# A two-layer block in one persistent loop: three of four state blocks summed by VectorE, taps read from PSUM, norms applied by ScalarE

## The reference, cut to what matters

```python
# layer 0: attention with squared scores (16 heads of 16), then an int8-weight FFN (hidden 768)
A = (q_i @ k_i.T) ** 2 * mask;  o = (inter + A @ v) / (inter_z + A.sum(-1) + EPS);  x = o @ Wo
h = silu(x @ wg) * (x @ wu);    x = h @ wd
# layer 1: a state-space part in two directions r (forward and reversed sequence), 512 channels, 16 states n
u  = silu(conv4(x @ Win_u) + convb)                 # a causal convolution with 4 taps along time
dt = softplus(dtr @ Wdt + bdt)
h_t[n] = exp(dt_t * A[n]) * h_{t-1}[n] + (dt_t * u_t) * B_t[n]
y_t    = sum_n h_t[n] * C_t[n];   y = (y + u * D) * silu(z);  out = y @ Wout
# and a block-FP4 quantised FFN (hidden 704)
```

## Time and profile before

| | us |
|---|---|
| median of 3 runs (lowest, highest) | 6962.02 (6948.84, 6964.09) |
| the profiled execution, its span | 6966.85, 6965.1 |
| busy in the span: VectorE, TensorE, GpSimd, ScalarE | 5281.2, 5063.0, 4972.3, 4022.4 |
| share of the span: VectorE, TensorE, GpSimd, ScalarE | 76%, 73%, 71%, 58% |
| mean granted clock of TensorE | 0.803 |
| transfers: mean, share of the 16 DMA engines for the main queue | 44 GB/s, 13.5% |

### The profile page before, as it was taken

How to read it: one execution, slowest core, us unless ns; L and a number is a source line. 1 busy time by engine, 2 the same in 40 slices (tenths; PEclk the granted TensorE clock), 3 DMA queues, 4 the chain that set the end, 5 groups by cost and what they waited for, 6 DMA issues and landing times.

```text
span 6965.1 us, 83507 instructions
## 1 busy us (share of the span) xinstructions
PE 5063.0 (73%) x21853; PEld 3220.5 (46%) x21900; DVE 5281.2 (76%) x6580; ACT 4022.4 (58%) x6424; POOL 4972.3 (71%) x3786
## 2 busy tenths in 40 slices
PE   3776777868777686877868777676877768777665
PEld 2344444544444444544444444444544444444444
DVE  3277788787878778788787878878787787878884
ACT  1365665656656565655656656565665656656563
POOL 0177877777777777777778777777777777777894
PEclk6688888878878788887878878788887878888777
DMA  3011111111111111111111111111111111111110
GB/s 107 25 36 40 43 48 49 34 50 43 39 50 50 44 34 44 45 48 50 45 43 39 38 51 48 45 33 44 47 48 48 47 43 38 40 48 45 37 46 25
DMA packets 152821, 309.07 MB, mean 44 GB/s; under 512 B 20870, under 2 KB 58310, under 8 KB 149926
## 3 DMA queue, kind: packets, MB, share of 16 engines
q1 hardware_dynamic: 152278, 302.80, 13.5%
HBM read 285.90 MB, written 16.84 MB: 43 GB/s over the span
## 4 chain that ended last, share of the span: by engine, by line
PE 32%; issue 21%; DVE 17%; POOL 17%; ACT 10%; DMA 0%; DVEq 0%; POOLq 0%; SPq 0%; ACTq 0%
POOL arena_m L714 7%; PE psum L1310 7%; PE psum L1501 6%; DVE arena_m L1216 5%; POOL arena_m L725 5%; PE psum L1354 3%; DVE arena_m L1227 2%; PE psum L1273 2%; PE psum L1443 2%; PE psum L1481 2%; ACT hc L931 2%; ACT L759 2%; PE psum L1417 2%; PE psum L1389 1%; DVE arena_m L1156 1%
## 5 line engine op out<-in xcount | busy, mean ns | idle before, releaser
L714 POOL TENSOR_TENSOR arena_m<-bS,arena_m 128x512 f32<-128x512 f32 x2048 | 2703.6, 1334 | 394.7 <-PE psum L1501 358.7
L1216 DVE TENSOR_TENSOR_SCAN arena_m<-psum,arena_m 128x512 f32<-128x512 f32 x2048 | 2452.0, 1209 | 138.4 <-POOL arena_m L714 58.0
L923 ACT ACTIVATE psum<-arena_m,Aneg 128x512 f32<-128x512 f32 x2048 | 1414.8, 694 | 1387.1 <-DVE arena_m L1216 1355.7
L1501 PE MATMUL psum<-ident,arena_m 128*128 128x128 f32 x8192 | 1491.2, 317 | 858.2 <-DVE arena_m L1227 643.5
L725 POOL TENSOR_TENSOR arena_m<-arena_m,hc 128x512 f32<-128x512 f32 x1024 | 1362.9, 1331 | 821.1 <-ACT hc L931 766.5
L1501 PEld LDWEIGHTS psum<-ident,arena_m 128*128 128x128 f32 x8192 | 1121.2, 162 | 1563.4 <-issue 601.3
L1227 DVE SCALAR_TENSOR_TENSOR arena_m<-psum,Ct,arena_m 128x512 f32<-128x512 f32 x1024 | 746.4, 729 | 286.2 <-PE psum L1501 261.3
L1310 PE MATMUL psum<-arena_a 64*128 64x512 f32 (+3 forms) x2048 | 789.0, 517 | 98.7 <-ACT arena_a L790 49.3
L931 ACT ACTIVATE hc<-psum,Ct 128x512 f32<-128x512 f32 x1024 | 695.0, 679 | 229.4 <-PE psum L1501 172.8
L790 ACT ACTIVATE arena_a<-psum 128x384 f32<-128x384 f32 (+1 forms) x768 | 399.6, 526 | 356.1 <-PE psum L1310 352.4
L1310 PEld LDWEIGHTS psum<-arena_a 64*128 64x128 f32 x2048 | 382.9, 214 | 353.4 <-issue 217.1
(11 more groups left out here) (151 smaller groups left out, 7524.0 us busy)
## 6 DMA issues: line engine op xcount, KB each, us to landing
bS<-brow SPq DMA_DIRECT2D x512, 256.0 KB, 3.2
wB<-kept_B SPq DMA_DIRECT2D x16, 1408.0 KB, 6.8
wU<-kept_U SPq DMA_DIRECT2D x32, 512.0 KB, 4.3
wZ<-kept_Z SPq DMA_DIRECT2D x32, 512.0 KB, 4.5
wO<-kept_O SPq DMA_DIRECT2D x32, 512.0 KB, 4.8
wA<-kept_A SPq DMA_DIRECT2D x16, 768.0 KB, 7.0
wB<-kept_B SPq DMA_DIRECT2D x16, 768.0 KB, 4.2
wA<-kept_A SPq DMA_DIRECT2D x16, 640.0 KB, 4.0
```

Source lines behind the costliest of these rows:

```text
L714: pool.tensor_tensor(hb[s % HBS][:, m, :], bS[:, s % 2, :], du[r][:, m, :], ALU.mult).then_inc(m_dbu.sem, 1)
L923: act.activation(EB[j % EBS], dt[r][:, m, :], ACT.Exp, scale=Aneg[:, r, m, n:n + 1]).then_inc(m_dA.sem, 1)
L1216: dve.tensor_tensor_scan(v, EB[j % EBS], v, 0.0, ALU.mult, ALU.add).then_inc(m_scan.sem, 1)
L1501: ins = pe.transpose(HT[pos % 2][:, m * P:(m + 1) * P], hb[s % HBS][:, m, i * P:(i + 1) * P], ident[:, :])
```

## The change

1. *Blocks.* `ORDER` is gone; blocks 0, 1 and 2 of a state are added by VectorE from bank `i % 2`, block 3 is weighted by ScalarE and added by GpSimd.
2. *Taps.* The convolution has no `upad`. The taps read the PSUM bank of the product directly, shifted in the output, and the bank is free when the taps are done.
3. *Softplus.* Abs and Exp work in place in the PSUM bank, and VectorE's correction reads it there; the bank is free when that is done. `du` is made by GpSimd behind its two sums.
4. *Norms.* VectorE makes scale and shift ([128, 4] each), and ScalarE applies them, four instructions each.
5. *Query masks.* ScalarE makes all four. Both query products stand two batches ahead; the second is copied to `qraw` and masked in steps 27 and 28 (`a_qmask`).
6. *Table.* Most side work has new steps.

```diff
-    ORDER = (0, 2, 1, 3)
-        for j0, r, ahead, outs, res in ((0, 1, -1, (8, 9, 10, 11), (10, 12)), (HALF, 0, 0, (72, 74, 76, 78), (75, 79))):
+        for j0, r, ahead, outs, res in ((0, 1, -1, (8, 9, 10, 11), (10, 12)), (HALF, 0, 0, (74, 75, 77, 78), (76, 79))):
...
-        row("a_wo", None, 1, PE=[53, 54], DVE=[54, 55])
+        row("a_wo", None, 1, PE=[55, 56], DVE=[57, 58])
...
-        row("f_rest", None, 1, DVE=[60, 60, 61, 61])
+        row("f_rest", None, 1, DVE=[65, 65, 66, 66])
...
-            row("q_up", None, -1, first=2 * i, PE=[j + 3, j + 4], DVE=[j + 4, j + 5])
+            row("q_up", None, -1, first=2 * i, PE=[j + 3, j + 4], DVE=[j + 4, j + 6])
...
-        row("a_q", None, 2, PE=[125], ACT=[126], DVE=[126])
-        row("a_q", None, 1, first=1, PE=[28], ACT=[29], DVE=[29])
+        row("a_q", None, 2, PE=[125, 126], ACT=[126, 127])
+        row("a_qmask", None, 1, ACT=[27, 27, 28, 28])
...
+        for j0, j, r, ahead in ((13, 30, 1, 0), (97, 107, 0, 1)):
+            late = (0, 3, 6, 9) if r else (0, 2, 4, 6)
+            row("p_in", r, ahead, PE=[j0 + c for c in late], ACT=[j0 + c + 1 - r for c in late])
+            row("p_conv", r, ahead, DVE=[j0 + c + 2 - r for c in late for k in range(PAD)])
+            row("p_silu", r, ahead, ACT=[j0 + late[-1] + 4 - r])
+            late = (4, 7, 10, 13) if r else (4, 5, 6, 7)
+            row("p_dt", r, ahead, PE=[j + c for c in late], ACT=[j + c + 1 - r for c in late], DVE=[j + c + 2 - r for c in late],
+                POOL=[j + c + 3 for c in late])
...
-            "p_in": (1, lambda r, n: [(m_up, 2 * (NM * r + n + 1))]), "p_x": (2, lambda r, n: [(m_xd, r + 1)]),
-            "p_c": (1, lambda r, n: [(m_ct, r + 1)]), "p_dt": (1, lambda r, n: [(m_rl, NM * r + n + 1)]),
+            "p_in": (1, lambda r, n: [(m_conv, PAD * (NM * r + n + 1))]), "p_x": (2, lambda r, n: [(m_xd, r + 1)]),
+            "p_c": (1, lambda r, n: [(m_ct, r + 1)]), "p_dt": (1, lambda r, n: [(m_c2, NM * r + n + 1)]),
...
+                pool.wait_ge(*m_sum.by(b, 2 * q + 2))
+                pool.tensor_tensor(du[r][:, m, :], dt[r][:, m, :], u[:, m, :], ALU.mult).then_inc(m_du.sem, 1)
...
+            def norm(b, n, src, dst):
+                act.wait_ge(*ln_scale[n].by(b, 4))
+                for i in range(NT):
+                    act.activation(dst[:, i, :], src[:, i, :], ACT.Identity, scale=rstd[:, n, i:i + 1],
+                                   bias=shift[:, n, i:i + 1]).then_inc(ln_out[n].sem, 1)
...
-                act.activation(ex[:, c, :], src, ACT.Abs, bias=bdt[:, r, m:m + 1]).then_inc(m_ab.sem, 1)
+                act.activation(src, src, ACT.Abs, bias=bdt[:, r, m:m + 1]).then_inc(m_ab.sem, 1)
...
-                dve.scalar_tensor_tensor(u[:, m, :], upad[:, m % 2, tap:tap + T], convw[:, r, m, tap:tap + 1], u[:, m, :],
+                dve.scalar_tensor_tensor(u[:, m, late:T], src[:, 0:T - late], convw[:, r, m, tap:tap + 1], u[:, m, late:T],
                                          ALU.mult, ALU.add).then_inc(m_conv.sem, 1)
...
-                dve.scalar_tensor_tensor(yT[:, i, :], HT[0], Ct[:, r, i, n:n + 1], yT[:, i, :], ALU.mult,
+                dve.scalar_tensor_tensor(yT[:, i, :], HT[i % 2], Ct[:, r, i, n:n + 1], yT[:, i, :], ALU.mult,
                                          ALU.add).then_inc(m_y.sem, 1)
...
-                    if j % 2:
-                        yb, jy = spot(b, j - 5)
-                        if exists(yb):
-                            add_state(yb, jy // 2)
+                    yb, jy = spot(b, j - 5)
+                    if jy % NT < NT - 1 and exists(yb):
+                        add_state(yb, jy)
...
-                if pos % 2 == 0:
-                    pe.wait_ge(*m_y.by(b, c // 2))
+                if i == 1:
+                    pe.wait_ge(*m_hc.by(b, s))
                 else:
-                    pe.wait_ge(*m_hc.by(b, c // 2))
+                    pe.wait_ge(*m_y.by(b, 3 * s + (0, 0, 1, 2)[i]))
```

More of the change, by code:

```diff
@@ new lines, in block_kernel @@
+        row("a_wo", None, 1, PE=[55, 56], DVE=[57, 58])
+        row("f_stat", None, 1, DVE=[58, 59, 59], ACT=[60])
+        row("f_norm", None, 1, DVE=[61], ACT=[62])
+        row("f_turn", None, 1, PE=[63, 63], ACT=[64, 64])
+        row("f_rest", None, 1, DVE=[65, 65, 66, 66])
+        row("f_gate", None, 1, PE=[67, 67, 68, 68, 69, 70], ACT=[68, 68, 69, 69, 70, 71])
+        row("f_silu", None, 1, ACT=[70, 72])
+        row("f_up", None, 1, PE=[71, 72, 73, 74, 75, 76], DVE=[73, 73, 74, 75, 76, 77])
@@ L309, in block_kernel @@
+        row("f_down", None, 1, PE=[78, 80, 82, 84], DVE=[81, 86])
+        row("m_stat2", None, 1, DVE=[82, 86, 86], ACT=[87])
+        row("m_norm2", None, 1, DVE=[88], ACT=[89])
+        row("m_stat3", None, 1, DVE=[90, 90, 90], ACT=[91])
+        row("m_norm3", None, 1, DVE=[92], ACT=[93])
+        row("m_x", None, 1, POOL=[91])
+        row("m_turn", None, 1, PE=[94, 94], ACT=[95, 95])
         row("q_stat", None, -1, DVE=[20, 22, 23], ACT=[26])
-        row("q_norm", None, -1, DVE=[62, 63])
@@ new lines, in block_kernel @@
+            row("q_hquant", None, -1, first=QHEAD * i, DVE=[j + 6, j + 6, j + 6, j + 7, j + 7, j + 8])
+            row("q_htail", None, -1, first=QTAIL * i, POOL=[j + 8, j + 9, j + 9])
+            row("q_hturn", None, -1, first=2 * i, PE=[j + 10, j + 10], ACT=[j + 11, j + 11])
+            row("q_down", None, -1, first=i, PE=[j + 12], DVE=[j + 13])
+        for j, r, ahead in ((30, 1, 0), (107, 0, 1)):
+            row("p_x", r, ahead, PE=[j, j + 1], ACT=[j + 2])
+            row("p_rows", r, ahead, SP=[j + 3])
+            row("p_c", r, ahead, PE=[j + 4], DVE=[j + 5])
@@ L348, in block_kernel @@
-        row("a_v", None, 2, PE=[122, 123], DVE=[123, 124])
-        row("a_q", None, 2, PE=[125], ACT=[126], DVE=[126])
-        row("a_q", None, 1, first=1, PE=[28], ACT=[29], DVE=[29])
-        row("a_weigh", None, 1, PE=[j + 5 for j in UNIT])
+        row("a_k", None, 2, PE=[121, 122], ACT=[122, 123])
+        row("a_v", None, 2, PE=[123, 124], DVE=[125, 126])
+        row("a_q", None, 2, PE=[125, 126], ACT=[126, 127])
+        row("a_qmask", None, 1, ACT=[27, 27, 28, 28])
+        row("a_weigh", None, 1, PE=[j + 5 + (gu % NU == 0) for gu, j in enumerate(UNIT)])
@@ L778, in attn_q, with attn_qmask @@
                 act.wait_ge(*a_q_ps.by(b, h + 1))
-                for j in range(2):
+                if h:
+                    act.copy(qraw[:, :], bank("a_q", None, h)).then_inc(a_qr.sem, 1)
+                    return
+                for j in range(G):
                     act.activation(qm[:, j, :], bank("a_q", None, h), ACT.Copy, scale=qmask[:, j:j + 1]).then_inc(a_qa.sem, 1)
+            def attn_qmask(b, _, j):
+                act.wait_ge(*a_s_ps.by(b, NG * NU * G // 2 - G + j + 1))
+                act.wait_ge(*a_qr.by(b, 1))
+                act.activation(qm[:, j, :], qraw[:, :], ACT.Copy, scale=qmask[:, j:j + 1]).then_inc(a_qa.sem, 1)
             def square(b, _, w):
```

250 lines of the change are left out of this document (98 added, 152 removed).

## The result

| | us |
|---|---|
| before, median of 3 runs | 6962.02 (6948.84 to 6964.09) |
| after, median of 3 runs | 7215.55 (7205.03 to 7242.28) |
| after / before | 1.0377, 95% interval 1.0355 to 1.0399 |
| the profiled execution after, its span | 7242.28, 7240.5 |
| forecast | 6665, range 6440 to 6990 |

The forecast has the wrong sign. Of its rivals, "Slower: TensorE gets pinned to VectorE" gave 7200. That it came so near is in part luck. One of its terms, TensorE's waits for banks held by VectorE, came out as priced. But the waits for the VectorE sum, which were to grow, shrank, and those for the weighing, which were to shrink, grew.

A forecast was written before the change was run, and what follows sets the result against it. No single engine was taken as the bound: each stretch by its fullest engine, plus 61.1 us of coupling per batch. Span 6965.1 - 240 (stretches) - 55 (attention output wait) = 6670, median 6665; range 6440 to 6990.

The forecast's parts named there:

- Taps: Convolution taps read from PSUM: 143 us off VectorE, bounds 0 to 172.
- Slower: TensorE gets pinned to VectorE: Rival, chance 0.17: in steps 13 to 50 TensorE waits more for VectorE, which now releases PSUM banks; 7200 us.
- TensorE's waits for banks held by VectorE: In the slower rival: convolution and softplus banks held by VectorE, 19.6 us per batch, 303 over 15.5 batches.
- The rest of the 61 us per batch I leave as it is: Engines waiting for each other in steps of one or two instructions: 61.1 us per batch, unchanged except at the attention output.
- -92: In the slower rival: TensorE's 183.4 us of waits for ScalarE's weighing fall by 92, with one weighing per state, not two.
- Stretches: Eight parts of a batch, 16 steps each; fullest engine taken again after load changes: -15.5 us per batch, -240 in all.
- The -55 for the attention output: VectorE's 109.2 us wait before the residual of the attention output: half saved by more room, -55 us.
- TensorE "nothing": TensorE's total load doesn't change; its busy time was to stay within 2% of 5063 us.
- Three blocks: Each of 512 states moves one block to VectorE: VectorE +371 us, GpSimd -681, ScalarE -348.
- Softplus constant step: VectorE's plus-one-minus-one in the softplus, read from PSUM instead of SBUF: +19 us, bounds 0 to 40.
- Norms on ScalarE: VectorE loses 184.7 us and gains 59; ScalarE gains 160, 0.5 per instruction, taken as hidden.
- What I named as a sign of the slower case: In the new profile: TensorE's waits for the VectorE sum above 900 us, or score products waiting for taps.

The follow-up runs named there:

- e1: The changed kernel with ScalarE's weighing of block 3 one step earlier (transpose plus 1 instead of plus 2); 6805.93 us, ratio 0.9781.
- e11: The kernel before with three of four blocks summed by VectorE, weighing at its old step, du made by GpSimd and norms applied by ScalarE; 6647.74 us.
- e5: The kernel before with three of four blocks summed by VectorE and ScalarE's weighing of the fourth at its old step; 6748.84 us, ratio 0.9707.
- e8: The changed kernel with the weighing one step earlier and the taps read from SBUF again, after a ScalarE copy; 6825.74 us, ratio 0.9810.
- e10: The kernel before with three of four blocks summed by VectorE, weighing at its old step, and norms applied by ScalarE; 6687.91 us, ratio 0.9616.
- e3: The changed kernel with the old division of blocks, two of four summed by VectorE and two by GpSimd; 6916.43 us, ratio 0.9934.

## Why the prediction was wrong

**The step that failed** is "The rest of the 61 us per batch I leave as it is", and in the rival the term "-92" with its reason, "Against it: the sum that frees a bank still stands one step number ahead of the transpose that wants it, as before". That holds for VectorE's sum (c+5). It doesn't for ScalarE's weighing, which went from c+5 to c+6. I had counted one weighing in place of two as less waiting: 183.4 to about 92. It became 682.8, with half as many weighings. The 61 us that were left as they are became 81.5. The code showed the later step: the index arithmetic of both kernels gives the step number of every weighing, and so does the order of the instructions. I checked it for VectorE only.

Point by point:

- *Coupling.* Fullest engines of the eight stretches after: 33.03 + 54.51 + 59.15 + 34.25 + 43.08 + 38.60 + 45.32 + 44.62 = 352.6, so of 434.1 us 81.5 are coupling, against 61.1 before. In e1 it is 71, in e11 58.4 (334.1 of 392.5). Of the 32.6 us per batch by which the forecast of the stretches is wrong (next point), 20.4 are coupling; the other 12.2 are fullest engines with more busy time than forecast, TensorE in stretches 2 and 3 above all.
- *Stretches.* Forecast 0, -3.6, 0, -6.7, +0.6, -4.4, -7.0, +5.6, sum -15.5. Measured +1.9, +12.2, +16.0, -4.3, +4.8, -7.3, -4.9, -1.3, sum +17.1. The method holds for 4, 6 and 7, where VectorE led, to within 3 us each. It fails in 2 and 3, where a fullest engine was taken as a fixed load. It also fails in 8, the other way: GpSimd was to be fullest there with 49.5 and has 40.27. 32.6 us times 15.5 is 505 us of the 570 by which the forecast misses the profiled span (7240.5 against 6670). The -55 for the attention output account for most of the rest. That wait did go as hoped, from 109.2 us to 7.5 (L1077 now), but no gain in time can be seen for it.
- *TensorE "nothing".* It rose by 253 us, +5%, outside the 2% that I had named as the test. The score products alone (L1310, now L1297) went from 789.0 to 931.3 us for the same 2048. This is no new work: their shortest and longest are the same (0.269 and 1.22 us), and the median went from 0.482 to 0.562. More of them ran at the lower clock level, as the granted clock of stretches 2 and 3 says.
- *Three blocks.* 383 us more for VectorE (746.4 to 1129.5) where 371 were forecast: right. By itself, with the weighing in step c+5, it saves 206 us (e5 against 6955.31).
- *Taps.* Right in the duration, as the rows for L1155 and L1169 after show (ns min/median/max):

```profile
L1155 DVE SCALAR_TENSOR_TENSOR arena_m<-psum,convw,arena_m x384: 735/748/752, 314.1 to 6880.8; 128x509 f32<-128x509 f32 x64, 128x511 f32<-128x511 f32 x64, 128x510 f32<-128x510 f32 x64
...
L1169 DVE TENSOR_SCALAR arena_m<-psum x128: 668/692/693, 336.8 to 6934.2; 128x512 f32<-128x512 f32 x128
```

  1.098 us on average became 0.748 (421.3 to 286.9 us), and the longest went from 6.881 to 0.752. e8 against e1 (mean 1.202 and 0.747) shows the same with only ScalarE's copies added. The rule of the Trainium skill (SBUF — State Buffer, Who interferes with whom) is borne out: without a second SBUF input no tap is blocked. The time for it is another matter: 20 us or nothing (e8). That TensorE was busy beside most of the taps may be why; no run tests it.
- *Softplus constant step.* I gave +19 us, its mean was 0.678 before (median 0.560) and is 0.687 now, so +1. I took the median as the basis of a group with a long tail, and for the price from PSUM I divided the busy time of the masks by their number (0.705), which is below the mean of one that the same row gives (0.746). The rule that fp32 from PSUM has no fast mode (the Trainium skill, VectorE: DVE Perf Modes, Why PSUM operands drop a tier) agrees with minimum 0.393 before and 0.668 now; but the blocked instructions of before had cost as much as the slower mode does.
- *Step sizes on GpSimd.* 1.270 us each, as forecast (1.345 in e11, where the taps read SBUF). Worth 12 us alone, within the noise, and 40 once the norms are gone from VectorE.
- *Norms on ScalarE.* 0.59 us each instead of 0.5. Worth 61 us by itself (e10), where VectorE is 162 us lighter; my sum had 185 - 59.
- *GpSimd.* 180 us less than forecast: products 2586.4 instead of 2703.6 us, sums 1.272 instead of 1.331. Fewer two-input instructions of VectorE leave its own shorter (e1 against e8 shows it for the taps: 2578.8 and 2632.4 us), which I had left out.
- *What I named as a sign of the slower case* was over 900 us of TensorE's waits for VectorE. It was 323.9. The sign looked at the wrong engine. The other, "score products waiting for taps", came with 55.7 us. All waits for banks held by VectorE came to 324 us, 302 more than before; the 303 that this rival put on them were right. But e3 and e1 have as much of them and are faster than before, so they alone didn't make the change slower.

The account of the 254 us, by runs: the third block with early weighing -206, everything else in the change +57 (e5 to e1), the weighing one step late +410; sum +261. Taken in another order it is: everything else -41 (e3), the third block -110 (e3 to e1), the weighing +410; sum +259. Either way the late weighing is more than the whole loss. What the other parts are worth depends on the order: beside two blocks per state on VectorE they gain 41 us, beside three they lose 57.

## What to carry to other kernels

Where two engines hand a small ring back and forth in program order, write down for each handover the step in which it is made and the step in which it is wanted, for every reader, and treat "same step" as an error: one step here is worth 250 to 410 us of 7000, where moving the third block was worth 110 to 206. A balance of busy times only holds where this slack is kept. When a change moves load and slack together, run the one-digit neighbours (one step earlier, one later) before judging the load; and look at TensorE's granted clock behind a wait as well as at the wait.
